# The response of the second half through the 32 columns of U: reduce each batch to four stacked copies of z, then one product with four stacked bands of rows

## What is computed

```
U_o, V_o = gram_schmidt(U), gram_schmidt(V)        # 256 x 32 each
basis    = U_o @ V_o.T
proj     = hid @ basis
feats    = proj @ basis.T[:, :32]
response = feats @ resp_w.T + resp_b + safety_bias
out      = hid + strength * response
```

## Time and profile before

| | us |
|---|---|
| median of 3 runs | 1367.18 (1366.38 to 1367.87) |
| profiled execution | 1369.96 |
| its span | 1367.8 |
| PE busy | 1321.2 (97%) |
| DVE busy | 1075.3 (79%) |
| ACT busy | 1071.8 (78%) |
| POOL busy | 871.5 (64%) |
| mean granted TensorE clock | 0.987 of full speed |

### The profile page before, as it was taken

The page is one execution under the profiler, slowest core; times in us unless marked ns, Lnnn a source line. Parts: engine busy times, 40 slices in busy tenths (PEclk is TensorE's granted clock), DMA queues, the critical chain, the costliest instruction groups (busy, mean ns, idle before and its releaser), DMA issues. The chain is left out here.

```text
span 1367.8 us, 39618 instructions
## 1 busy us (share of the span) xinstructions
PE 1321.2 (97%) x11936; PEld 1119.3 (82%) x11936; DVE 1075.3 (79%) x3638; ACT 1071.8 (78%) x2664; POOL 871.5 (64%) x874
## 2 busy tenths in 40 slices
PE   4999999999999999999999998789999999999997
PEld 3777777777777777777777776579999999999997
DVE  4777777787877777778778777578888888888885
ACT  1788888888888888888888886777777777777773
POOL 4999989989999998998999998311222222122210
PEclk9999999999999999999999999989999999999998
DMA  9546656555564665655556482101010110111100
GB/s 289 184 152 200 191 161 207 166 188 181 169 210 152 197 191 159 208 164 187 181 169 210 154 259 70 32 24 40 31 46 31 35 42 31 46 31 41 36 24 32
DMA packets 182670, 175.07 MB, mean 128 GB/s; under 512 B 15552, under 2 KB 182112, under 8 KB 182624
## 3 DMA queue, kind: packets, MB, share of 16 engines
q1 hardware_dynamic: 181248, 173.64, 40.1%
q10 hardware_dynamic: 1376, 0.85, 0.2%
HBM read 157.69 MB, written 16.78 MB: 128 GB/s over the span
## 5 line engine op out<-in xcount | busy, mean ns | idle before, releaser
L428 POOL TENSOR_TENSOR ring<-ring,maskv 128x1024 f32<-128x1024 f32 x256 | 600.0, 2373 | 12.4 <-DMA ring<-in_fside 5.1
L912 ACT ACTIVATE ring<-ring,nmax 128x256 f32<-128x256 f32 x1024 | 452.5, 501 | 24.6 <-DVE nmax L606 24.6
L606 DVE CUSTOM_DVE_ANT_0 ring<-bank,ring 128x256 f32<-128x256 f32 x1024 | 373.0, 418 | 90.4 <-PE bank L1176 73.5
L917 ACT ACTIVATE pT<-bank 128x512 f32<-128x512 f32 x416 | 239.5, 592 | 103.5 <-PE bank L1191 103.4
L1191 PE MATMUL bank<-ident,ring 128*128 128x128 f32 x2048 | 292.6, 278 | 1.4 <-ACT pT L917 1.1
L1191 PEld LDWEIGHTS bank<-ident,ring 128*128 128x128 f32 x2048 | 231.9, 143 | 70.6 <-issue 47.9
L1047 ACT ACTIVATE work<-bank,b1t 128x256 f32<-128x256 f32 x256 | 107.6, 476 | 109.0 <-PE bank L1390 109.0
L1176 PE MATMUL bank<-work 32*128 32x256 f32 x2048 | 148.4, 404 | 6.0 <-DVE nmax L606 5.2
L1390 PE MATMUL bank<-hT_high,w_high 128*128 128x256 f32 x512 | 147.9, 289 | 3.4 <-DVE hT_rest L781 3.4
L1403 PE MATMUL bank<-w_high,gT_high 128*128 128x256 f32 x512 | 148.1, 289 | 0.0
L1403 PE MATMUL bank<-w_rest,gT_high 128*128 128x256 f32 x512 | 145.3, 284 | 0.0
(11 more groups left out here) (162 smaller groups left out, 2730.5 us busy)
## 6 DMA issues: line engine op xcount, KB each, us to landing
ring<-in_fside SPq DMA_DIRECT2D x128, 1024.0 KB, 7.7
xt<-in_x SPq DMA_DIRECT2D x32, 256.0 KB, 3.2
x_d<-x2s SPq DMA_DIRECT2D x32, 256.0 KB, 7.8
work<-x_d SPq DMA_DIRECT2D x32, 256.0 KB, 2.8
out<-pT SPq DMA_DIRECT2D x32, 256.0 KB, 2.2
mk<-in_mask SPq DMA_DIRECT2D x32, 64.0 KB, 6.7
w<-in_W SPq DMA_DIRECT2D x2, 1024.0 KB, 10.5
wada<-in_W_ada SPq DMA_DIRECT2D x1, 512.0 KB, 8.1
```

The lines of the kernel that those rows point to most:

```text
L428: nc.gpsimd.tensor_tensor(v, v, m, ALU.add).then_inc(s_masked, 1)
L606: nc.vector.tensor_tensor_reduce(out=v, in0=score_ps[h % HG][:, qt], in1=v, scale=-1.0, scalar=ROW_MAX_NEG, op0=ALU.add, op1=ALU.min, accu ...
L912: nc.scalar.activation(v, v, ACT.Exp, bias=nmax[:, b.par, h, qt:qt + 1], scale=-1.0).then_inc(s_exp, 1)
L917: nc.scalar.activation(pT[:, h % (2 * HG)], tp_ps[h % 2], ACT.Copy).then_inc(s_pta, 1)
```

## The change

M is no longer built. Per batch, `reduce_z` computes z = (U_o.T hid.T), 32 rows by 256, with a stationary operand in which the 32 columns of U_o stand four times side by side, so that four equal bands of 32 rows come out (6 matmuls). `z_high` copies all bands, rounded; `z_rest` overwrites bands 2 and 3 with the rest. The other factor t (32 x 256) is made once in four bands, high, rest, high, rest. One matmul of 128 contraction rows then gives all four part products (2 matmuls per batch). `reduce_z` writes to the second half of bank 6. The order on the engines changes as well:

```
 # TensorE
+def reduce_z(b):
     pe.wait_ge(s2_hidl, b.n + 1)
+    pe.wait_ge(s2_h1, b.n + 1)
+    ... wait_ge(s2_zl, b.n)
+    for c in range(DC):
+        for k, (kw, kx) in enumerate(HI_LO):
+            ins = mm(z_ps, us[kw][:, c], hidTs[kx][:, c], ...)
+    ins.then_inc(s2_zp, 1)
 def response(b):
+    pe.wait_ge(s2_zl, b.n + 1)
     for t in range(QT):
-        for c in range(DC):
-            for k, (kx, kw) in enumerate(HI_LO):
-                ins = mm(tiles2(5)[:, t], hidTs[kx][...], resp_ms[kw][:, c], ...)
+        ins = mm(tiles2(5)[:, t], zs[:, t * P:(t + 1) * P], ts, start=True, stop=True)
 # body2 of TensorE
     down(b.plus(-1), 0)
-    response(b.plus(-2))
+    reduce_z(b.plus(-2))
     up_pair(b, 2)
     down(b.plus(-1), 1)
+    response(b.plus(-2))
     up_pair(b, 3)
 # body2 of VectorE
     gate_pair(b, 1)
     gT_rest(b, 0)
+    gate_hidden(b.plus(-2))
     hT_rest(b.plus(1))
-    gate_hidden(b.plus(-2))
     gate_sum(b.plus(-2))
-    rsp_out(b.plus(-2))
+    z_rest(b.plus(-2))
     gate_pair(b, 2)
     ...
     strength(b.plus(-2))
+    rsp_out(b.plus(-2))
     fin_out(b.plus(-2))
 # body2 of ScalarE
     hT_out(b.plus(1))
+    z_high(b.plus(-2))
     tanh_pair(b, 2)
 # hid_transpose on TensorE also waits for s2_zl of the batch before
+def z_high(b):
+    act.wait_ge(s2_zp, b.n + 1)
+    nc.scalar.activation(zs, z_ps, ACT.Copy).then_inc(s2_zh, 1)
+def z_rest(b):
+    dve.wait_ge(s2_zh, b.n + 1)
+    nc.vector.tensor_tensor(zs[2*R:4*R], z_ps[2*R:4*R], f32(zs[2*R:4*R]), ALU.subtract).then_inc(s2_zl, 1)
 # between the halves: U's transposes, step 2, and the copies of U.T, t2 and M go;
 # the Gram matrix is copied out four times side by side, t comes straight in four bands;
 # U and t are split instead of M (2 operations on ScalarE, 3 on VectorE, for 1 and 1)
```

More of the change, by code:

```diff
@@ L141, in attention_block_kernel @@
         nrm = sb("nrm", [P, 2]); nrme = sb("nrme", [P, 2]); rnrm = sb("rnrm", [P, 2]); qcol = sb("qcol", [P, 2, DC]); gprod = sb("gprod", [P, 2, DC, R]); coef = sb("coef", [P, 2, R])
-        respT = sb("respT", [R, D]); gram = sb("gram", [R, R]); t1 = sb("t1", [R, D]); t2 = sb("t2", [R, D]); uoT = sb("uoT", [R, D]); resp_m = sb("resp_m", [P, DC, D])
+        respT = sb("respT", [R, D]); gram = sb("gram", [R, HG, R]); t1 = sb("t1", [R, D])
         ring = sb("ring", [P, RING, QT, CH, S])
@@ L173, in attention_block_kernel @@
         hidTs = [lay("hidT_high", [P, DC, S], xt_at), lay("hidT_rest", [P, DC, S], xt_at + 4 * DC * S)]
-        resp_ms = [lay("resp_m_high", [P, DC, D], xres_at), lay("resp_m_rest", [P, DC, D], xres_at + 4 * DC * D)]
+        us = [lay("u_high", [P, DC, P], xres_at), lay("u_rest", [P, DC, P], xres_at + 4 * DC * P)]
+        ts, zs = lay("t_parts", [P, D], xres_at + 4 * 2 * DC * P), lay("z_parts", [P, S], xres_at + 4 * (2 * DC * P + D))
         regions = [work[:], pT[:].rearrange("p h t s -> p (h t s)")]
@@ L210, in attention_block_kernel @@
         prep_ps = tiles2(7)
+        z_ps, t_ps = bank[6][:, S:2 * S], bank[5][:, 0:D]
         gs_ps = bank[7][:, 0:2 * R].rearrange("p (a r) -> p a r", a=2)
@@ L228, in attention_block_kernel @@
         s2_six = sem("s2_six"); s2_stats = sem("s2_stats"); s2_pool = sem("s2_pool"); s2_rstd = sem("s2_rstd"); s2_yb = sem("s2_yb"); s2_yn = sem("s2_yn")
-        s2_yt = sem("s2_yt"); s2_hT = sem("s2_hT"); s2_up = sem("s2_up"); s2_th = sem("s2_th"); s2_u = sem("s2_u"); s2_ua = sem("s2_ua"); s2_w = sem("s2_w"); s2_wl = sem("s2_wl"); s2_hf = sem("s2_hf"); s2_hl = sem("s2_hl"); s2_gh = sem("s2_gh"); s2_gl = sem("s2_gl"); s2_hidf = sem("s2_hidf"); s2_hidl = sem("s2_hidl"); s2_m = sem("s2_m"); s2_ml = sem("s2_ml"); s2_g = sem("s2_g"); s2_dn = sem("s2_dn")
+        s2_yt = sem("s2_yt"); s2_hT = sem("s2_hT"); s2_up = sem("s2_up"); s2_th = sem("s2_th"); s2_u = sem("s2_u"); s2_ua = sem("s2_ua"); s2_w = sem("s2_w"); s2_wl = sem("s2_wl"); s2_hf = sem("s2_hf"); s2_hl = sem("s2_hl"); s2_gh = sem("s2_gh"); s2_gl = sem("s2_gl"); s2_hidf = sem("s2_hidf"); s2_hidl = sem("s2_hidl"); s2_m = sem("s2_m"); s2_ml = sem("s2_ml"); s2_zp = sem("s2_zp"); s2_zh = sem("s2_zh"); s2_zl = sem("s2_zl"); s2_g = sem("s2_g"); s2_dn = sem("s2_dn")
         s2_hid = sem("s2_hid"); s2_hidp = sem("s2_hidp"); s2_hidT = sem("s2_hidT"); s2_r = sem("s2_r"); s2_h1p = sem("s2_h1p"); s2_h1 = sem("s2_h1"); s2_zs = sem("s2_zs")
@@ L581, in gs_reciprocal, with response_matrix @@
                 nc.vector.reciprocal(rnrm[:], nrme[:]).then_inc(s_grec, 1)
[L583 to L593, removed]
+            def response_matrix():
+                dve.wait_ge(s_rm, 1)
+                nc.vector.tensor_copy(gram[:], bank[0][0:R, 0:R].unsqueeze(1).to_broadcast([R, HG, R]))
+                nc.vector.tensor_copy(t1[:], bank[1][0:R, 0:D]).then_inc(s_rmc, 1)
             def reduce_head(b, h):
@@ L762, in body @@
                 if n == B:
-                    response_matrix(0)
+                    response_matrix()
                     split_weights(0)
-                    response_matrix(1)
-                    response_matrix(2)
             reduces(first, (0, 1, 2))
@@ L836, in hidT_rest @@
                 if b.i is not None or b.off >= 1:
-                    dve.wait_ge(s2_r, b.n)
+                    dve.wait_ge(s2_zp, b.n)
                 nc.vector.tensor_tensor(hidTs[1], hidT, f32(hidTs[0]), ALU.subtract).then_inc(s2_hidl, 1)
+            def z_rest(b):
+                dve.wait_ge(s2_zh, b.n + 1)
+                nc.vector.tensor_tensor(zs[2 * R:4 * R], z_ps[2 * R:4 * R], f32(zs[2 * R:4 * R]), ALU.subtract).then_inc(s2_zl, 1)
             def rsp_out(b):
@@ L856, in _ @@
             dve.wait_ge(s2_m, 1)
-            nc.vector.tensor_tensor(resp_ms[1], resp_m[:], f32(resp_ms[0]), ALU.subtract).then_inc(s2_ml, 1)
+            nc.vector.tensor_tensor(us[1].rearrange("p c (k r) -> p c k r", k=HG), uv[:, 0].unsqueeze(2).to_broadcast([P, DC, HG, R]),
+                                    f32(us[0]).rearrange("p c (k r) -> p c k r", k=HG), ALU.subtract)
+            for k in (1, 3):
+                rows = slice(R * k, R * (k + 1))
+                ins = nc.vector.tensor_tensor(ts[rows], t_ps[rows], f32(ts[rows]), ALU.subtract)
+            ins.then_inc(s2_ml, 1)
             def body2(b, n):
@@ L873, in body2 @@
                     gT_rest(b, 0)
+                if tail2:
+                    gate_hidden(b.plus(-2))
+                if main:
                     if n is None or n + 1 < B:
@@ L1065, in hidT_out @@
                 if b.i is not None or b.off >= 1:
-                    act.wait_ge(s2_r, b.n)
+                    act.wait_ge(s2_zp, b.n)
                     act.wait_ge(s2_h1p, b.n)
@@ L1073, in hidT_out @@
                 nc.scalar.activation(hidTs[0], hidT, ACT.Copy).then_inc(s2_hidT, 1)
+            def z_high(b):
+                act.wait_ge(s2_zp, b.n + 1)
+                if b.i is not None or b.off >= 1:
+                    act.wait_ge(s2_r, b.n)
+                nc.scalar.activation(zs, z_ps, ACT.Copy).then_inc(s2_zh, 1)
             def gate2(b):
@@ L1082, in _ @@
             split_weights(1)
-            act.wait_ge(s_rmc, 3)
+            act.wait_ge(s_rm, 2)
             act.wait_ge(s_x2, B)
-            nc.scalar.activation(resp_ms[0], resp_m[:], ACT.Copy).then_inc(s2_m, 1)
+            nc.scalar.activation(us[0].rearrange("p c (k r) -> p c k r", k=HG), uv[:, 0].unsqueeze(2).to_broadcast([P, DC, HG, R]), ACT.Copy)
+            nc.scalar.activation(ts, t_ps, ACT.Copy).then_inc(s2_m, 1)
             yn_out(Batch(1))
@@ L1153, in response_matrix @@
                         mm(bank[0][0:R, 0:R], uv[:, 1, c], uv[:, 1, c], start=(c == 0), stop=(c == DC - 1))
-                    mm(bank[1][0:R, 0:D], uv[0:R, 0, 0], respT[:], start=True, stop=True)
-                    for c in range(DC):
-                        ins = nc.tensor.transpose(bank[2][0:R, c * P:(c + 1) * P], uv[:, 0, c], ident[:])
+                    ins = mm(bank[1][0:R, 0:D], uv[0:R, 0, 0], respT[:], start=True, stop=True)
                 if step == 1:
                     pe.wait_ge(s_rmc, 1)
[L1159 to L1163, removed]
+                    ins = mm(t_ps, gram[:].rearrange("p k r -> p (k r)"), t1[:], start=True, stop=True)
                 ins.then_inc(s_rm, 1)
@@ L1364, in body @@
                     pv(b, 2)
-                if n == B:
-                    response_matrix(2)
             run_batches(pe, 0, 3, B - 3, B + 1, body)
@@ L1372, in _ @@
             pe.wait_ge(s_x2, B)
-            pe.wait_ge(s_rmc, 3)
             def up_pair(b, j):
@@ L1411, in hid_transpose @@
                     pe.wait_ge(s2_h1, b.n)
+                    pe.wait_ge(s2_zl, b.n)
                 for c in range(DC):
@@ L1421, in gate_h1 @@
                 ins.then_inc(s2_h1p, 1)
+            def reduce_z(b):
+                pe.wait_ge(s2_hidl, b.n + 1)
+                pe.wait_ge(s2_h1, b.n + 1)
+                if b.i is not None or b.off >= 1:
+                    pe.wait_ge(s2_zl, b.n)
+                else:
```

(14 more changed lines are left out.)

## The result

The changed kernel takes 1494.84 us (median of 4 runs, 1493.67 to 1495.99) against 1366.99 us (4 runs, 1366.38 to 1367.87). The ratio is 1.0935 with a 95% interval of 1.0916 to 1.0954: 128 us slower, where 1492 us were forecast. The profiled execution took 1495.99 us with a span of 1493.8 us and a mean clock of 0.945.

The account below looks back on a forecast made before the run. TensorE's own stream was taken to bound the second half. Against the profiled execution: 1370.0 - 15.0 + 78.8 + 3.3 + 60 - 1.5 = 1495.6 us; for the runs 1492 us, 8-in-10 range 1430 to 1520.

Parts of the forecast that it names:

- The matmuls that go: TensorE, second half: response's 12 matmuls become 8, saving 0.47 us for each batch, -15.0 us over 32 batches.
- The wait: TensorE before reduce_z: a 2.67 us stall for VectorE's gate_hidden, 78.8 us in sum, plus 3.3 us for slower first matmuls.
- the ring: up_pair 3, ScalarE 4.2 us, VectorE 5.0 + 0.2 us, reduce_z, TensorE's rest: no slack, so the stall returns every iteration.
- The clock: TensorE behind the new pauses: granted clock falls in nearly every batch, 2.0 us each, 30 batches, 60 us.
- the row at 898.93: First up_pair of the second half: after 2.18 us idle the clock was at 0.55; 24 matmuls took 2.6 us more.
- the pause of 1.23 us: TensorE before 909.26 in the old profile: the clock stayed at 1.00, giving the clock term's lower bound of 0.
- Rival A: TensorE's clock stays at 2.4 GHz behind the new pauses: 1433 us; chance 0.16.
- Rival B: The clock falls in only some batches, costing 10 to 40 us: 1443 to 1473 us; chance 0.13.
- The new evictions at nothing: z_high on ScalarE, z_rest and moved rsp_out on VectorE: costed at nothing, -0.2 to +0.5 us for each batch.
- Between the halves: Step 2 and its copies go, so the second half's first up_pair starts earlier: -1.5 us (0 to -2.2).
- Rival D: gate_hidden on VectorE is in time, so the four matmuls of each batch are won: 1351 us; chance 0.06.

Follow-up runs that it names:

- the versions without the pause: Changed kernel with reduce_z writing to bank 5, without its wait for gate_hidden (1354.19 us), and changed kernel with gate_hidden right behind hidT_rest (1352.58 us).
- `gate_hidden` earlier: Changed kernel, all waits kept, gate_hidden right behind hidT_rest in VectorE's order, ahead of stats2 and gate_pair 1: 1352.58 us, ratio 0.9894.
- both with needless matmuls in the pause: Changed kernel with 18 or 10 needless matmuls between down 0 and reduce_z's wait for gate_hidden: 1444.75 us with 18, 1441.15 us with 10.
- `gate_hidden` late: Changed kernel with gate_hidden left behind hT_rest on VectorE, as in the kernel before: 1501.29 us, ratio 1.0976.
- the other bank: Changed kernel with reduce_z writing to the first half of bank 5, waiting for the previous batch's rsp_out instead of gate_hidden: 1354.19 us, ratio 0.9911.
- the kernel with the wait alone: Kernel before, 12 matmuls per response, but response also waits for gate_hidden, which stands ahead of hT_rest: 1479.28 us, ratio 1.0829.
- four needless matmuls: Changed kernel with 4 needless matmuls right behind the 6 of reduce_z, z_high released behind them: 1486.89 us, ratio 1.0876.

## Why the prediction was right

**The matmuls that go.** 0.47 us for each batch was forecast; the versions without the pause have a period 0.49 us shorter. The new products cost what the old ones do.

**The wait.** 2.67 us was forecast, 2.58 and 2.93 in turn (2.76 in the mean) were measured. The argument that nothing in the ring has slack, so that the pause returns in every iteration, held: VectorE's run to `gate_hidden` was 5.01 us again, and 16.59 us for the ring at full clock stand against 14.16 - 0.47 + 2.67 + 0.11 = 16.47. Why every second pause is 0.2 to 0.35 us longer was not tried; VectorE's and TensorE's loops take two batches in a turn, which would fit. In iterations 30 and 31 the pauses were 1.56 and 1.93 us against the 2.0 taken.

**The clock.** 2.0 us for each batch was forecast, 2.2 measured, and 60 us in all against 54 or a little more. That the clock would fall in nearly every batch was right; that the size came out was in good part luck. The row that put the term there, the fall behind 1.74 us near the end, is no rule. A pause of the same 1.74 us, between the same two steps (`hid_transpose` and `gate_h1`), stands in all nine profiled kernels. The clock fell behind it in six (the kernel before, the changed one, `gate_hidden` earlier, both with needless matmuls in the pause, `gate_hidden` late) and stayed in three. With the other bank, and with `gate_hidden` earlier (timeline of TensorE and busy times of each):

```profile
1332.74 0.66 PE L1426 MATMUL bank<-gw,pooled 128*128 128x64 f32 x4 [1.74 <-ACT pT L1076]
1332.70:1336.00 3.30, 3.26 (x27) 3.26 (x28) 2.64 (x7) 1.15 (x2) 0.00 (x0) 1.00 0.10 34
```
```profile
1329.48 0.66 PE L1425 MATMUL bank<-gw,pooled 128*128 128x64 f32 x4 [1.74 <-ACT pT L1075]
1331.00:1333.00 2.00, 2.00 (x12) 2.00 (x11) 1.31 (x5) 0.00 (x0) 0.00 (x0) 0.50 0.00 0
```

In a trace where the clock stayed there, only the row at 898.93 would have spoken for a fall. Nor was the pause of 1.23 us behind which it stayed a bound: the regular pauses of 1.4 to 1.6 us never cost the clock, and one of 2.59 us once did not. Rival A, that the clock stays, was wrong for this kernel, but its 1433 us was near the kernels with filled pauses: 1441 and 1445. Rival B, a fall in only some batches, is what the kernel with the wait alone does. The advice of the Trainium skill (TensorE: Matmul & The Clock Gate, "Why this matters for your kernels") is to avoid idle gaps longer than ours; read as a rule that shorter ones are harmless, it did not hold here: pauses of 2.58 us were enough in all but one batch of the changed kernel. For the regular pauses near 1.5 us that reading held.

**The new evictions at nothing.** Right. `z_high` takes 0.38 us, `z_rest` 0.43, and no idle time stands before `response` in any of the kernels with the new products, except 0.94 us in the last iteration. There the prediction left out some 0.1 us: from the start of the last `hidT_rest` to that of the last `fin_out` it is 4.24 us now (1486.19 to 1490.43) for 3.87 (1360.57 to 1364.44).

**Between the halves.** -1.5 us was forecast. By the timelines of TensorE the first `up_pair` now starts 6.83 us after attention's last output projection (888.15 to 894.98) where it took 9.21 (889.72 to 898.93): 2.4 us; with the other bank it is 7.18 (889.65 to 896.83), 2.0 us. The runs can't confirm that: the two versions without the pause are 12 and 14 us below the kernel before, and the shorter periods alone make 15 or 16. Some 3 us of gain are missing in them. The profiled spans are 17 and 18 us apart, but the kernel before was profiled in an execution 3 us over its median. Where the 3 us are stays open.

**The other side.** Rival D priced the change without its pause at 1351 us and named the point on which it turns, whether VectorE's `gate_hidden` ends before TensorE's last matmul of `down` 0. Moved there, it gave 1352.58.

## What to carry to other kernels

A wait that looks free, because the two steps stand in the same iteration on both engines, has to be laid on the clock times of the old trace: where in its round is the releasing engine when the waiting one arrives? Where an engine is busy without a gap, a pause in its stream is paid in full and again in every iteration, and a reordering by one operation or a PSUM bank that nobody else holds is worth more than the arithmetic saved. One pause in an old trace does not price the clock behind a new one: here the same pause of 1.74 us cost it in six kernels and not in three, so such a term wants a range that starts at nothing. If a regular pause can't be removed, try filling it.

## What the runs showed of the hardware

- Whether the granted clock falls behind a pause does not hang on the pause's length alone. Behind regular pauses of 2.6 to 3.0 us it fell in 27 of 28 iterations of the changed kernel, whose ring is 16.6 us at full clock. With 0.47 us more matmuls on the ring it fell in 15 of 28 (the wait alone) and in 18 of 28 (four needless matmuls). With pauses of 3.2 and 3.5 us it fell in 27 of 28, at less cost each. Behind the regular pauses of 1.4 to 1.6 us it never fell. What decides was not found. More work on the ring made the kernel faster by 8 us, needless work in the pause by 54 us.
- `fin_out`, 128x512 out of SBUF into SBUF on VectorE, took 1.56 us in the kernel before while GpSimd's `add_b2` (1.29 us) ran beside it, and 1.00 us in the changed one, where it begins later against it. `rsp_out`, whose first input is in PSUM, now begins beside `add_b2` and is not slowed. From VectorE's and GpSimd's timelines of the kernel before, and then of the changed kernel:

```profile
1105.22 1.56 DVE L852 SCALAR_TENSOR_TENSOR pT<-pT,strg,work 128x512 f32<-128x512 f32 x1 [0.24 <-DVE strg L831]
```
```profile
1104.94 1.29 POOL L474 TENSOR_TENSOR work<-work,b2b 128x512 f32<-128x512 f32 x1 [4.12 <-DVE work L812]
```

```profile
1233.48 0.68 DVE L842 TENSOR_TENSOR pT<-bank,cb 128x512 f32<-128x512 f32 x1
1234.36 1.00 DVE L850 SCALAR_TENSOR_TENSOR pT<-pT,strg,work 128x512 f32<-128x512 f32 x1 [0.20 <-DVE pT L842]
```
```profile
1233.53 1.28 POOL L476 TENSOR_TENSOR work<-work,b2b 128x512 f32<-128x512 f32 x1 [7.74 <-DVE work L805]
```

  With `rsp_out` moved there VectorE gets back some 0.56 us for each batch, more than `z_rest` costs it. It is off the path here, and the cause was read from the timelines, not tried.
